# Regrouping the small matmul groups and the VectorE queue of the steady pairs in a fused attention kernel

## The reference, cut to what matters

```
# 1. cross block: both operands fake-quantised to 8 bits (round, clip to 0..255, shift, scale)
x = x + matmul(fake_quant(layernorm(x)), fake_quant(ctx))        # ctx: 16 x 1024 x 1024
# 2. causal self attention, 32 heads of 32, rotary positions on q and k
q, k, v = split(layernorm(x) @ qkv_w + qkv_b)
x = x + softmax(rope(q) @ rope(k).T / sqrt(32) + causal) @ v @ out_w + out_b
# 3. linear layer plus 16 weighted rank-16 updates
x = x + layernorm(x) @ W.T + bias + sum_e c_e * (layernorm(x) @ A_e.T) @ B_e.T
```

## Time and profile before

| | |
|---|---|
| time, median of 3 runs | 609.09 us (608.94 to 610.46) |
| profiled execution | 609.3 us, span of the records 606.8 us |
| granted TensorE clock, mean | 1.0 of full speed |
| TensorE matmul busy | 587.5 us, 97% of the span |
| VectorE busy | 459.5 us, 76% |
| ScalarE busy | 293.1 us, 48% |
| GpSimd busy | 125.2 us, 21% |

### The profile page before, as it was taken

One profiled execution on the slowest core, in us unless ns is written; L12 is line 12 of the kernel. 1 busy time (PEld: TensorE's weight loads), 2 busy tenths in 40 slices (PEclk: granted clock), 3 DMA queues, 4 the chain that ended last, 5 costly groups with the idle time before them and its releaser, 6 DMA issues.

```text
span 606.8 us, 12924 instructions
## 1 busy us (share of the span) xinstructions
PE 587.5 (97%) x4922; PEld 291.9 (48%) x4922; DVE 459.5 (76%) x903; ACT 293.1 (48%) x359; POOL 125.2 (21%) x173
## 2 busy tenths in 40 slices
PE   3899999999999999999999999999999999999998
PEld 1354454455545445554455445545455554444445
DVE  6699997788767966787677868677864788987751
ACT  5888795865456435644553464546331242310100
POOL 4000010000256225513541354345100000000000
PEclk9999999999999999999999999999999999999999
DMA  8999996751465165507631663365322026477541
GB/s 324 386 387 396 391 385 223 262 208 71 144 205 210 70 224 195 194 12 277 219 127 60 216 242 104 119 200 200 104 83 92 1 74 239 120 142 174 139 103 53
DMA packets 53713, 111.82 MB, mean 184 GB/s; under 512 B 18602, under 2 KB 18986, under 8 KB 53680
## 3 DMA queue, kind: packets, MB, share of 16 engines
q1 hardware_dynamic: 37760, 104.35, 48.6%
q10 hardware_dynamic: 15648, 6.48, 5.0%
q0 software_dynamic: 272, 0.55, 0.2%
HBM read 99.30 MB, written 8.39 MB: 177 GB/s over the span
## 4 chain that ended last, share of the span: by engine, by line
PE 84%; DVE 9%; SPq 2%; issue 2%; DMA 2%; ACT 1%; DVEq 0%; ACTq 0%
PE dense L1370 14%; PE dense L1372 14%; PE dense L1371 14%; PE turn L1361 5%; PE dense L1582 4%; PE dense L1583 4%; PE dense L1584 4%; PE dense L1840 4%; DVE wq L956 4%; PE cross L1430 3%; PE score L1543 3%; PE dense L1598 2%; PE cross L1415 2%; PE dense L1843 2%; DMA wq<-in_ctx 2%
## 5 line engine op out<-in xcount | busy, mean ns | idle before, releaser
L1370 PE MATMUL dense<-wq,xn_h 128*128 128x512 f16 x376 | 143.1, 380 | 0.5 <-DVE at L1040 0.2
L1371 PE MATMUL dense<-wq,xn_h 128*128 128x512 f16 x376 | 142.5, 379 | 0.0
L1372 PE MATMUL dense<-wq,xn_l 128*128 128x512 f16 x376 | 142.5, 379 | 0.0
L822 POOL TENSOR_TENSOR acc<-code,acc 128x256 int32<-128x256 int32 x140 | 103.9, 770 | 115.0 <-ACT code L381 114.6
L381 ACT ACTIVATE code<-raw,cst,qc 128x1024 uint8<-128x1024 f32 x72 | 87.4, 1237 | 14.5 <-DMA raw<-in_ctx 13.3
L1370 PEld LDWEIGHTS dense<-wq,xn_h 128*128 128x128 f16 x376 | 36.7, 98 | 46.6 <-issue 12.7
L1372 PEld LDWEIGHTS dense<-wq,xn_l 128*128 128x128 f16 x376 | 36.8, 98 | 44.4
L381 ACT ACTIVATE code<-lnt,cst,qc 128x1024 uint8<-128x1024 f32 x32 | 39.6, 1238 | 28.3 <-DMA lnt<-in_ctx 27.8
L1371 PEld LDWEIGHTS dense<-wq,xn_h 128*128 128x128 f16 x376 | 36.9, 98 | 32.2
L1017 DVE SCALAR_TENSOR_TENSOR at<-cst,score 128x512 f32<-128x512 f16 x24 | 16.4, 684 | 40.0 <-PE score L1543 40.0
L1582 PE MATMUL dense<-wo,rope 128*128 128x512 f16 x112 | 42.5, 379 | 0.8 <-DVE rope L1047 0.8
(11 more groups left out here) (242 smaller groups left out, 1041.6 us busy)
## 6 DMA issues: line engine op xcount, KB each, us to landing
raw<-in_ctx SPq DMA_DIRECT2D x72, 512.0 KB, 4.4
lnt<-in_ctx SPq DMA_DIRECT2D x32, 512.0 KB, 4.2
wo<-in_ctx SPq DMA_DIRECT2D x16, 512.0 KB, 9.5
wo<-in_qkv_w SPq DMA_DIRECT2D x12, 512.0 KB, 11.5
wq<-in_qkv_w SPq DMA_DIRECT2D x8, 512.0 KB, 12.2
x_scratch<-xa SPq DMA_DIRECT2D x8, 512.0 KB, 3.0
wo<-in_out_w SPq DMA_DIRECT2D x7, 512.0 KB, 6.7
wq<-in_ctx SPq DMA_DIRECT2D x6, 512.0 KB, 11.7
```

What stands on the lines that cost most here:

```text
L822: ins = pool.tensor_tensor(sums[:, cols], words[:, cols], acc_from.to_broadcast([P, half]) if c < 2 else sums[:, cols], ALU.add)
L1370: pe.matmul(bank[:, :], a_h[:, k, :], w_hi, start=(k == 0 and not started), stop=False)
L1371: pe.matmul(bank[:, :], a_h[:, k, :], w_lo, start=False, stop=False)
L1372: ins = pe.matmul(bank[:, :], a_l[:, k, :], w_hi, start=False, stop=(k == KC - 1 and not last))
```

## The change

In the steady pairs (and, for the step of the values, in pair 7):

- TensorE, `qkv(i, 2)`: the second cross group `t(2, 3)` goes from behind k = 7 to behind k = 6, directly after the first scores.
- TensorE, `qkv(i, 5)`: the fourth cross group `t(6, 7)` goes from behind k = 0 to behind k = 5; the shift goes from behind k = 6 to behind k = 5; the waits of `values_due` go from behind k = 3 to behind k = 4, and `values(i, 0)` from behind k = 4 to behind k = 5. Fourth group, shift and first values then stand in a row.
- VectorE: `v_sum(i, 0)` goes ahead of `softmax_in(i, 3)`; `sums_as_f16` goes ahead of `softmax_out(i, 2)`; `c_low(i, 0)` goes ahead of the two `tiled_evac`.

No instruction is added or removed.

```
                 w(30)
                 softmax_in(i, 2)
+                if not late:
+                    v_sum(i, 0)
                 softmax_in(i, 3)
...
                 else:
-                    v_sum(i, 0)
+                    sums_as_f16(i + 1)
                     softmax_out(i, 2)
-                    sums_as_f16(i + 1)
                     softmax_out(i, 3)
+                    c_low(i, 0)
                     tiled_evac(i + 1, 0)
                     tiled_evac(i + 1, 1)
-                    c_low(i, 0)
                     v_sum(i, 1)
...
-                    qkv(i, 2, {1: [at(t, 0, 1)], 3: [...], 4: [at(m, 1)], 6: [at(middle_biases, i), at(scores, i, 0)], 7: [at(t, 2, 3)]})
+                    qkv(i, 2, {1: [at(t, 0, 1)], 3: [...], 4: [at(m, 1)], 6: [at(middle_biases, i), at(scores, i, 0), at(t, 2, 3)]})
...
-                    qkv(i, 5, {0: [at(t, 6, 7)], 1: [at(m, 4)], 2: [at(m, 5)], 3: [at(values_due, i, 0)], 4: [at(values, i, 0)],
-                               6: [at(shifted), at(evacuated, i, 0), at(p_turn, i, 2)], 7: [at(p_turn, i, 3)]})
+                    qkv(i, 5, {1: [at(m, 4)], 2: [at(m, 5)], 4: [at(values_due, i, 0)], 5: [at(t, 6, 7), at(shifted), at(values, i, 0)],
+                               6: [at(evacuated, i, 0), at(p_turn, i, 2)], 7: [at(p_turn, i, 3)]})
```

More of the change, by code:

```diff
@@ L1770, in next_pair @@
                     qkv(i, 1, {3: [at(codes)], 5: [at(m, 0)], 6: [at(codes_turned, 0), at(qk_turn, i, 0)]})
-                    qkv(i, 2, {1: [at(t, 0, 1)], 3: [at(codes_turned, 1), at(qk_turn, i, 1)], 4: [at(m, 1)], 6: [at(middle_biases, i), at(scores, i, 0)], 7: [at(t, 2, 3)]})
+                    qkv(i, 2, {1: [at(t, 0, 1)], 3: [at(codes_turned, 1), at(qk_turn, i, 1)], 4: [at(m, 1)], 6: [at(middle_biases, i), at(scores, i, 0), at(t, 2, 3)]})
                 late = isinstance(i, int) and i == 1
```

## The result

The changed kernel takes 604.11 us (median of 4 runs, 603.86 to 605.4) against 609.08 us before; the ratio is 0.9918 with a 95% interval of 0.9905 to 0.9932. The forecast was 604.2 us in a range of 603.0 to 606.4.

What follows compares the result with a forecast made beforehand. TensorE was taken as the bound, with gain only in borders and stalls: 0.095 + 0.33 + 0.245 + 0.32 - 0.05 = 0.94 us a pair, 4.7 us over five, plus 0.25, giving 604.2 us, range 603.0 to 606.4.

Steps and rivals of the forecast that it cites:

- The bound: TensorE, busy 97% at full clock; only borders between tile shapes and stalls between its matmuls can be won.
- The joins: Cross group behind first scores saves 0.095 us; fourth group, shift and values in a row save 0.33 us a pair.
- the turn behind the shift: Transposes right behind the shift take 0.49 us instead of 0.44; that border goes too, 0.05 us in five pairs.
- The value sum and `c_low`: TensorE's stalls in the last value block (0.245 us) and before the projection (0.32 us) both go, each pair.
- The cast: VectorE's cast of the code sums is seen at 260.3, TensorE reaches the shift at 260.6: 0.3 us cover.
- What is late next: The next pair's new rows: `lnt` seen at 270.6, TensorE there at 270.7, a cover of about 0.1 us.
- The charge of 0.05 us a pair: Average loss assumed at TensorE's wait for the next pair's new rows, taken off the gain.
- rival B: VectorE's chain to the new rows becomes the bound, 0.3 us a pair lost, 605.7 us; chance 0.17.
- rival D: Nothing gained: time given back at the pair's end waiting for low halves, residual or codes, 609 us; chance 0.06.
- the four terms: Per pair: 0.095 us at the first scores, 0.33 in the row, 0.245 at the value sum, 0.32 at `c_low`.
- C: Joining gives nothing, every small group keeps its way in and out; only stalls are saved, 606.3 us; chance 0.11.
- E: Slower: the row of three groups hangs on a cast delayed by GpSimd's late sum, 612.9 us; chance 0.03.

Runs made afterwards that it cites:

- VectorE's order alone: The kernel before with the three moves in VectorE's queue and TensorE's old order: 606.75 us, ratio 0.9958.
- second group alone: The kernel before with only the second cross group moved directly behind the first scores: 608.89 us, ratio 0.9991.
- cast-late run: The changed kernel with the cast of the code sums back behind `softmax_out(i, 2)`: 610.06 us, ratio 1.0009.
- two-step run: The changed kernel with two more statistics operations on VectorE before the second norm of each steady pair: 607.09 us, ratio 0.9956.
- c_low late: The changed kernel with `c_low(i, 0)` back behind the two `tiled_evac`: 608.20 us, ratio 0.9978.
- third group moved: The changed kernel with the third cross group moved from k = 5 of block 3 to directly behind the second scores: 604.42 us, ratio 0.9915.
- fourth group apart: The changed kernel with the fourth cross group back behind k = 0, shift and values still in a row: 605.09 us, ratio 0.9934.
- TensorE's order only: The kernel before with TensorE's new order and VectorE's old one: 609.97 us, ratio 1.0010.
- one extra operation: The changed kernel with one more 128x512 statistics operation on VectorE before the second norm of each steady pair: 604.46 us, ratio 0.9919.

## Why the prediction was right

**The bound.** It stood on TensorE having idle time that the busy share hides and that the wait view shows at half its size (0.15 of 0.32 us at `c_low`) or not at all (the value sum in pairs 3 to 6), and on reading it from distances between starts. Both stalls were there, in every pair, and the run with VectorE's order alone gave back their sum, 0.57 us a pair, in three of four.

**The joins.** Forecast: 0.095 us at the first scores, 0.33 in the row and 0.05 at the turn behind the shift. Measured: 0.11 for the first (second group alone). In the row 0.95 us of gain from the second scores to the new rows, less 0.245 and 0.32 of stalls, is 0.38, as the two terms say. Of its joints, cross to shift is not free but costs 0.03 us; shift to values is 0.10, as taken.

**The value sum and `c_low`.** No stall remains at either. The value sum ends at 255.50 + 0.68 = 256.2 and TensorE passes its wait at 257.67, 1.5 us later, or 1.36 with a release of 0.13 taken off (1.3 forecast). `c_low` ends at 261.86 + 0.75 = 262.6, TensorE asks for it at 263.23: 0.5 us of cover with the release taken off (0.3 forecast).

**The cast.** It ends at 258.14 + 0.69 = 258.83, the shift starts at 259.30: 0.47 us, 0.42 with the 0.05 us taken off that TensorE needed after the cast in the cast-late run; 0.3 was forecast. The cast-late run shows the price beyond it: the excess itself, once a pair.

**What is late next.** The new rows, as forecast, with 0.14 us of cover (0.1 forecast). The charge of 0.05 us a pair was paid only in pair 5, with 0.09 us. There the chain was 15.78 us long, 0.20 more than in the pairs before; the forecast had said that B decides from about 15.8. So rival B came true in one pair of five and at the size of its margin; the two-step run shows that a longer chain would have been paid in full. GpSimd's adds met the same step of the statistics as before, 0.54 and 0.53 us.

**A wait that was not in the forecast.** In every pair the first turn of q and k needs VectorE's rotation of that block (L1009), which stands in its queue behind the early statistics and the row codes. Before the change this turn was 0.16 us late in pair 2 and had 0.05 to 0.6 us of cover in pairs 3 to 6, so rival D's "TensorE now shows no stall there" was not right for pair 2. How late the rotation ends changes from pair to pair, as the steps before it do: the one at L874 takes from 0.16 to 0.69 us in the changed kernel. The turn was 0.17 us late in pair 2 of the changed kernel and 0.01 in pair 5, 0.30 in pair 3 of the VectorE run, 0.18 in pair 5 of the second-group run, 0.17 in pair 4 of "c_low late" and 0.43 in pair 4 of "third group moved", and each time what follows it lost 0.05 us more. These waits are the odd distances behind the medians of the table. For the forecast they were small: the four terms and the turn behind the shift give 1.04 us a pair, which is what a pair gains where nothing waits (57.24 to 56.20), and the small waits of both kinds take 0.04 of it in the mean, against a charge of 0.05.

**The other rivals.** C (joins give nothing) falls by the first table rows: joins are 0.43 of the 1.00 us a pair, if one takes the VectorE run's 0.57 off, and by the run with the fourth group apart. D (given back at the pair's end) falls by the distances of 56.2 us. E did not occur, and the cast-late run shows what a late cast costs.

The sum was 4.9 us against 4.97 measured (609.08 to 604.11), so near that chance has a part in it: single runs of one kernel differ by 1.5 us here. That the charge at the new rows and the waits met instead come to the same size is luck too.

## What to carry to other kernels

On a saturated TensorE look at start-to-start distances, not at busy shares: a quarter of a microsecond per wait and a tenth per change of tile shape repeat in every loop pass, and the wait view showed here one of the two stalls at half its size and of the other and the borders nothing. Before joining small groups, ask what each of them waits for. Where it is there early, as at the first scores, the join pays by itself (0.11 us); where it is not, as in the last value block, it has to be moved forward in its own producer's queue too, or the consumer waits as long as it saved (here 0.11 us a pair longer in all). After each such step write down the cover of the next waits (0.14 us at the new rows, 0.4 at the cast, and at the rotation between nothing and 0.7), look at all pairs and not at one, and reorder every queue that feeds them before the next step.

## What the runs showed of the hardware

- A group of small matmuls costs TensorE 0.095 us going in and 0.12 us coming out when the tile shape changes between it and dense matmuls; between two groups of one shape 0.03 us, between 128 x 64 and 64 x 32 tiles 0.10 us.
- TensorE went on 0.13 to 0.15 us after the end of the VectorE operation that released it, for the value sum, `c_low` and `lnt`. Behind the cast it was 0.05 us, in the cast-late run (262.12 - 262.07) and in the run with TensorE's order only, and behind the rotation 0.06 (287.60 - 287.54). Why they differ, no run shows.
- A turn of four that started late, or straight behind the shift, held TensorE 0.49 us instead of 0.44; a turn of eight that started late 0.93 instead of 0.88.
- A 128 x 1 step of VectorE with both inputs in SBUF took 0.53 us while GpSimd added and 0.16 us otherwise; in the changed kernel it ends at 267.14 + 0.54 = 267.68, with GpSimd's adds (265.34 + 2.32 = 267.66). Steps of 128 x 512 with both inputs in SBUF took 1.10 and 1.15 us instead of 0.69 while GpSimd added. From 156 to 450 us of the changed kernel's profile 24 steps of the lines L874, L875, L877, L1009 and L1023 are more than 0.15 us longer than their shortest, and all 24 overlap GpSimd's adds. The Trainium skill (SBUF — State Buffer, section on the two separate sides) describes such a lock between the two engines, held for a whole instruction; the run with one extra operation agrees with it, since the step became short as soon as it started behind the adds. Work put in front of such a step can be almost free: 0.60 us cost 0.09 us a pair.
